# Two-layer graph kernel: eight weighted sums per graph, from eight single places to two bursts of four

## What is computed

```python
# layer 0
hi = x @ W1[:H];  hj = x @ W1[H:]
h  = relu(hi[i, None, :] + hj[None, j, :] + b1)       # 128 x 128 pairs of 128 values
y  = layernorm(h @ W2 + b2) * gamma + beta            # one row of 128 for every pair (i, j)
out[i] = sum_j adj[i, j] * y[i, j, :]                 # the weighted sums
x  = layernorm(x + out)
# layer 1
Wh = x @ W_w.T + W_b
s  = (Wh @ a_w[:C])[i] + (Wh @ a_w[C:])[j] + a_b
e  = exp(s) * adj;  alpha = e / e.sum(j)
x  = layernorm(x + alpha @ x)
```

## Time and profile before

| What | us |
|---|---|
| median of 3 runs | 2303.24 |
| lowest and highest of them | 2301.99, 2304.12 |
| the profiled execution, its own time | 2303.22 |
| its span in the trace | 2301.4 |
| granted clock of PE, mean over the span | 0.998 of full speed |
| busy in the span: PE, PEld | 2280.2, 2075.6 |
| busy in the span: ACT, DVE, POOL | 2160.9, 2145.2, 2016.9 |

### The profile page before, as it was taken

The page is one execution under the profiler, slowest core; times in us unless marked ns, Lnnn a source line. Parts: engine busy times, 40 slices in busy tenths (PEclk is TensorE's granted clock), DMA queues, the critical chain, the costliest instruction groups (busy, mean ns, idle before and its releaser), DMA issues.

```text
span 2301.4 us, 168989 instructions
## 1 busy us (share of the span) xinstructions
PE 2280.2 (99%) x71248; PEld 2075.6 (90%) x71248; DVE 2145.2 (93%) x18262; ACT 2160.9 (94%) x3650; POOL 2016.9 (88%) x1227
## 2 busy tenths in 40 slices
PE   8999999999999999999999999999999999999997
PEld 8888888888888999999999999999999999999995
DVE  7999999999999999999999999999999999999998
ACT  8999999999999999999999999999999999999996
POOL 9898898888988988888888898898888988888884
PEclk9999999999999999999999999999999999999999
DMA  1000000000000000000000000000000000000000
GB/s 21 12 13 16 11 16 16 10 16 12 15 16 10 16 16 11 16 12 15 16 11 16 13 13 16 11 16 16 10 16 13 14 16 10 16 17 10 16 10 10
DMA packets 103862, 32.15 MB, mean 14 GB/s; under 512 B 77888, under 2 KB 103104, under 8 KB 103104
## 3 DMA queue, kind: packets, MB, share of 16 engines
q1 hardware_dynamic: 102240, 21.12, 4.4%
q10 hardware_dynamic: 864, 0.23, 0.0%
HBM read 17.11 MB, written 4.19 MB: 9 GB/s over the span
## 4 chain that ended last, share of the span: by engine, by line
PE 97%; ACT 2%; DVE 1%; POOL 0%; issue 0%; DMA 0%; SPq 0%; DVEq 0%; ACTq 0%
PE y_ps L567 76%; PE agg_ps L618 19%; PE work_ps L567 2%; ACT h L294 1%; ACT y L289 1%; POOL h L278 0%; DVE squares L553 0%; DMA b1c<-in_L_gnn_b_dram 0%; DVE o_sb L465 0%; DVE x_out L545 0%; POOL wz L269 0%; SPq L172 0%; DVE work_ps L483 0%; DVE work_ps L530 0%; DVE work_ps L479 0%
## 5 line engine op out<-in xcount | busy, mean ns | idle before, releaser
L278 POOL TENSOR_TENSOR h<-abT 128x1024 f32<-128x1024 f32 x1024 | 1944.0, 1919 | 239.3 <-PE y_ps L567 231.9
L567 PEld LDWEIGHTS y_ps<-w_pair,h 128*32 128x32 f32 x65536 | 1920.4, 110 | 173.6 <-issue 126.5
L567 PE MATMUL y_ps<-w_pair,h 128*32 128x128 f32 x65536 | 1966.0, 273 | 1.3 <-issue 0.6
L553 DVE CUSTOM_DVE_ANT_0 squares<-y_ps,y 128x128 bf16<-128x128 f32 x8192 | 1839.0, 284 | 110.4 <-ACT y L289 103.4
L289 ACT ACTIVATE y<-y_ps 128x508 f32<-128x508 f32 x2048 | 1137.5, 596 | 104.6 <-PE y_ps L567 97.6
L294 ACT ACTIVATE h<-h 128x1024 f32<-128x1024 f32 x1024 | 1089.3, 1064 | 2.4 <-POOL h L278 2.4
L553 DVE DVE_READ_ACCUMULATOR2_ANT q<- 128x1 f32 x8192 | 678.5, 83 | 0.0
L618 PE MATMUL agg_ps<-y,wz 128*32 128x512 f32 x4096 | 593.4, 592 | 3.2 <-DVE work_ps L483 3.1
L618 PEld LDWEIGHTS agg_ps<-y,wz 128*32 128x32 f32 x4096 | 180.4, 110 | 9.1 <-issue 9.1
L567 PEld LDWEIGHTS work_ps<-x1s,adjS 128*32 128x32 f32 x512 | 28.4, 110 | 31.5 <-issue 18.9
L252 POOL TENSOR_TENSOR wz<-adjT,rstd 128x128 f32<-128x128 f32 x64 | 34.8, 543 | 25.0 <-ACT rstd L325 25.0
(11 more groups left out here) (87 smaller groups left out, 591.3 us busy)
## 6 DMA issues: line engine op xcount, KB each, us to landing
adj_in<-in_adj_dram SPq DMA_DIRECT2D x256, 16.0 KB, 1.9
x_res<-in_x_dram SPq DMA_DIRECT2D x64, 64.0 KB, 2.1
adj_res<-in_adj_dram SPq DMA_DIRECT2D x64, 64.0 KB, 2.7
out_dram<-x_out SPq DMA_DIRECT2D x64, 64.0 KB, 1.9
x_in<-in_x_dram SPq DMA_DIRECT2D x254, 16.0 KB, 1.9
w1a<-in_L_gnn_W_dram SPq DMA_DIRECT2D x1, 64.0 KB, 1.9
w1b<-in_L_gnn_W_dram ACTq DMA_DIRECT2D x1, 64.0 KB, 2.2
w<-in_L_gnn_W_dram ACTq DMA_DIRECT2D x1, 64.0 KB, 2.3
```

The lines of the kernel that those rows point to most:

```text
L278: nc.gpsimd.tensor_tensor(h[:, u % HRING].rearrange("k (r g) s -> k r g s", g=GROUPS), abT[:, p, 1, :].unsqueeze(1).unsqueeze(1).broadcast ...
L553: last = nc.vector.tensor_tensor_reduce(out=squares[:, (first_bank + k) % YRING, n, :], in0=y_ps[(first_bank + k) % YRING][:, n, :], in1=y ...
L567: last = nc.tensor.matmul(dst[cols], lhsT[:, cols], rhs, start=start, stop=stop, tile_position=(0, g * GROUP))
```

## The change

The eight sums of a slot stand in two bursts: chunks 0 to 3 behind unit 8, chunks 4 to 7 behind unit 15, in every slot, the last ones too. `sums_behind` and the two constants are gone. What `prep_products` does is as it was; since it stands ahead of unit 9, its products now follow the first burst directly. No instruction is added or taken away on any engine, only PE's order is another, and no wait is added. From line 60 on the lines of the changed kernel have lower numbers: L566 and L611 below are L567 and L618.

```diff
--- before.py
+++ after.py
@@ -56,8 +56,7 @@
     CHUNK = 4
     CHUNKS = GROUP // CHUNK
     POOL_WEIGHTS_UNIT, POOL_RESIDUAL_UNIT = 5, 6
-    SUMS_HELD = 10
-    SUM_AT = {u: c for c, u in enumerate((4, 6, 7, 9, 10, 12, 13, 15))}
+    SUMS_BEHIND = {8: range(0, 4), 15: range(4, 8)}
 
     ctx = ExitStack()
     with ctx:
@@ -604,12 +603,6 @@
             mm(setup_ps[:, 3, 0:1], replicated(wbc), a1c[:], stop=False)
             mm(setup_ps[:, 3, 0:1], replicated(wbc), a2c[:], start=False).then_inc(s_setup_pe, 1)
 
-            def sums_behind(t, u):
-
-                if t == B - 1 and u > SUMS_HELD:
-                    return range(SUM_AT[SUMS_HELD] + 1, CHUNKS) if u == UNITS - 1 else ()
-                return (SUM_AT[u],) if u in SUM_AT else ()
-
             def weighted_sums(b_parity, chunk):
 
                 y_chunk = y[:, b_parity, chunk * CHUNK * GROUPS:(chunk + 1) * CHUNK * GROUPS, :].rearrange(
@@ -649,7 +642,7 @@
                             for n in range(QUART):
                                 last = mm(y_ps[(first_bank + k) % YRING][:, n, :], h[:, u % HRING, (k % QPU) * QUART + n, :], w_pair[:])
                             last.then_inc(y_in_psum, 1)
-                    for chunk in sums_behind(t, u) if gather else ():
+                    for chunk in SUMS_BEHIND.get(u, ()) if gather else ():
                         if chunk == 0:
 
                             pe.wait_ge(w_ready, t)
```

## The result

The changed kernel takes 2330.45 us, the median of 4 runs (2328.35 to 2333.99), against 2303.68 us before: a ratio of 1.0119, 95% interval 1.0107 to 1.0132. Slower was right, but 10.5 us were forecast and 26.8 came, and 2330 lies above the range of 2308 to 2324.

A forecast was written before the change was run, and what follows sets the result against it. PE was taken as the bound, its own work filling slots of 35.47 us. A stall at unit 8 (9.9 us) plus slot 1 (0.6) made 10.5 us on 2303.2: 2313.7 us, 0.5% slower, range 2308 to 2324.

The forecast's parts named there:

- What bounds the kernel: Slots 2 to 63: PE's own work fills 35.47 us without waits, but for a few idle stretches up to 0.8 us.
- Part one: Sums and products in every slot: regrouping leaves PE's work the same, 0 us, with 4 us either way.
- Part two: Unit 8, each slot: PE arrives before its relu ends and stalls 0.16 us, 9.9 us over 62 slots.
- short form: ACT's chain to the relu of unit 8, as in slot 3: ends 14.06 us after slot start, not 14.21.
- Unit 7 just passes: Start of unit 7: its relu ends at 124.83, PE is free at 124.92, so no wait.
- The bank: Quarters 14 to 16: squares free banks 0.12 to 0.16 us early; a late release would make the stall about 0.26.
- Part three: Slot 1, unit 8: without the three sums ahead PE waits for its relu, +0.6 us.
- Part four: Behind both bursts: ACT and DVE drain, but PE needn't wait for them afterwards, 0 us.
- Part five: End of the program, slot 64: moves by the stall alone, any wait there below 0.1 us, counted as 0 us.
- a longer stall for the relu: Rival, unit 8: 0.26 to 0.33 us a slot, 2320 to 2324 us; chance 0.25.
- the drained pipeline: Rival, behind a burst: the refill holds PE up, 0.5 us a slot adding 31 us, 2345; chance 0.04.
- A price of changing kind: Rival, switches between sums and products: cost PE time, 0.027 us each cancels the stall, 0.06 gives 2291; chance 0.04.

The follow-up runs named there:

- e2: Changed kernel with four bursts of two sums, behind units 4, 8, 11 and 15, no stretch longer than five units; 2303.7 us.
- e7b: Changed kernel with the Ln and Exp of the weights moved on ACT behind the relu of unit 8; 2330.5 us.
- e1: Changed kernel with its bursts of four sums behind units 7 and 15, two stretches of eight units; 2324.7 us.
- e5: Kernel before with a met wait added on PE for every node, 8192 more instructions; 2594.1 us.
- e3: Changed kernel with one sum behind each unit from 8 to 15, no burst, the stretch of nine units kept; 2328.8 us.
- e4: Changed kernel with one sum of the first burst put back behind unit 4, the stretch of seven units kept; 2310.7 us.
- e9: Kernel before with a met wait added on PE for one node of each quarter, 2048 more instructions; 2318.8 us.
- e8: Changed kernel with the loads of x, adj and residuals cut to a quarter of their bytes, same places and waits; 2329.1 us.
- e10: Changed kernel with three bursts, behind units 5, 11 and 15, and stretches of six, six and four units; 2308.5 us.

## Why the prediction was wrong

- **What bounds the kernel**: right as far as it went. Slots of 35.47 are PE's own work. But the sentence "but for a few with one idle stretch of up to 0.8 us" named the thing that decided, and went by it. These pieces were written off as rare. They stood at block starts, nearly all of their time in units 4 and 6, at the end of the stretch of five units and two units on, and the change makes that stretch nearly twice as long.
- **Part one, the work itself, 0 us**: the price of grouping was right (e2, and bursts of 3.43 us). The step that failed is here: "all its own work" was taken to cost the same however long products go on. It costs 19.0 us more than before, because PE's code comes late in stretches of nine and seven units; no term of the sum and no rival held that.
- **Part two, the relu of unit 8, +0.16 a slot**: the mechanism and the size were right to 0.01 us where it acted (14.07 after the slot's start, released in 0.05, in the short form as chosen). It acted in 36 slots and not in 62, since late code held PE up first in nearly all the others: 5.8 us instead of 9.9. "Unit 7 just passes" was not quite so: in 21 slots it waited too, some 0.07 us each. The bank was never the last to be waited for.
- **Part three, slot 1**: 0.6 forecast, 0.8 found.
- **Part four, behind the bursts, 0 us**: right for ACT, DVE and POOL. "Does anything give it back? No" held, but the same question asked the other way, what else does a stretch without sums use up, wasn't asked.
- **Part five, the end**: 0.0 forecast, 0.5 found; a late block of 0.29 us stands in it, just ahead of slot 63's last sums.
- **The rivals**: the range's upper end came from a longer stall for the relu, which didn't occur; the drained pipeline was close in size (31 us) and wrong in place, as PE's idle pieces are ahead of the bursts, not behind them. A price of changing kind, 0.027 to 0.06 us each, is shown by no run: four sums in a burst take 3.43 us, 0.86 each, as one between two units does, and e2, with four changes less in a slot, takes 2303.7 like the kernel before.

The sum from the runs: 19.0 (code) + 5.8 (relu) + 0.8 + 0.5 = 26.1, the difference of the spans. The 19.0 is what the others leave of it. e7b, without a relu's wait, gives it by itself: 21.7 - 2.9 = 18.8. The direction was forecast rightly in part by luck, as only about a quarter of the loss has the cause that was named.

What is shown: the idle pieces are at one instruction in each 256 (after, e1, e5, e7b), they end some 1.4 us after their packet of code has ended (after, e1, e5), they follow the length of the stretch without sums and not the burst (e2, e3, e4), they grow with the code (e5, e9), and neither the relu (e7b) nor the data loads (e8) make them. That sums refill a reserve is read from the lead of the packets, which is longest behind sums in both kernels. What stays open: why a late block took 4.4 us in e5 and 3.9 in the kernel after. Between two late blocks that follow each other (199 such pairs in e5, 10 in the kernel after) the packet takes about as long (median 1.17 and 1.11 us), and so does the time from its end to the block's first instruction (1.40 and 1.39); what differs is how long after a block's first instruction the next packet starts, 1.75 us in e5 and 1.41 in the kernel after. Why that is longer isn't shown.

## What to carry to other kernels

Short matmuls use up code fast: here 256 instructions in 3.47 us, and a stretch of more than five such units (8.7 us) was enough for PE to wait for its own program, 4.9 us in all with six (e10) and 18.8 with nine and seven. The long matmuls set between them were time for the code to come in: in the kernel after it was 1.5 us ahead in unit 7 and 3.7 in unit 9, behind the burst. So spread them even where the arithmetic doesn't ask for it; groups of two were still free (e2, 2303.7 us). Idle pieces by "issue" in the middle of a run of equal instructions are to be counted in instructions from one to the next before they are called rare: here the distance of 256, with a packet of code that ended some 1.4 us before each, marked the blocks of code.

## What the runs showed of the hardware

- PE's code came in packets of 16 KB, 561 for 143,775 instructions, so 256 in each, which is also the distance of the idle pieces. It was not always there in time: PE stood still at block starts for 2.9 us in the kernel before, 18.8 in the kernel after and 282 in e5.
- A late block's first instruction started 1.4 us after the end of its packet (median 1.42 in the kernel after, 1.41 in e1, 1.39 in e5), and the packet itself took 1.1 us.
- A wait that had long been met was not free on PE: 8192 of them cost 290.9 us, 35.5 ns each (e5), 2048 cost 14.9 us, 7.3 ns each (e9). The price isn't the instruction's own: quarters without a block start took 0.873 us with these waits and without. It lies at block starts, 282.1 us of it in e5 and 12.6 in e9, and it is higher where a slot has more blocks: 9.27 in e5 and 8.89 in e9, against 8.77 in the kernel before.
